# Message layer: destinations, and edge features of five tiles a group, held in PSUM

## The reference, cut to what matters

```
msg  = relu(x[src] + edge_attr)                 # 100000 x 96
aggr = segment_sum(msg, dst, num_segments=3125)
h    = x + aggr
h    = relu(h @ W1 + b1) @ W2 + b2
return x + relu(h)
```

## Time and profile before

| | us |
|---|---|
| median of three runs | 3176.62 |
| profiled execution | 3170.49 |
| its span | 3168.8 |
| first to last indirect gather of the message layer (starts) | 1474.7 to 2173.4 |
| GpSimd busy in those 539 gathers | 535.6 |
| VectorE busy between 1600 and 1700 us | 86.7 |
| TensorE busy in the same 100 us | 93.8 |

### The profile page before, as it was taken

The page is one execution under the profiler, slowest core; times in us unless marked ns, Lnnn a source line. Parts: engine busy times, 40 slices in busy tenths (PEclk is TensorE's granted clock), DMA queues, the critical chain, the costliest instruction groups (busy, mean ns, idle before and its releaser), DMA issues.

```text
span 3168.8 us, 72113 instructions
## 1 busy us (share of the span) xinstructions
PE 2675.9 (84%) x25058; PEld 2208.0 (70%) x25059; DVE 2367.4 (75%) x6307; ACT 640.5 (20%) x1255; POOL 1206.4 (38%) x1205
## 2 busy tenths in 40 slices
PE   4677777889999997996999999997689888888884
PEld 1222222789999997995999999997567677666663
DVE  7888877853332356448888888887799999999986
ACT  0011222510000005011111111111233333333331
POOL 0000000000000000003777777773477777777771
PEclk9999999899999998997999999998799999999996
DMA  1000000000000000003544444441333333333330
GB/s 30 0 0 0 0 0 0 2 1 2 2 1 2 2 2 5 2 1 81 130 120 117 119 116 117 119 115 38 95 103 107 102 107 108 104 104 109 102 98 19
DMA packets 108153, 180.74 MB, mean 57 GB/s; under 512 B 36346, under 2 KB 69900, under 8 KB 107867
## 3 DMA queue, kind: packets, MB, share of 16 engines
q0 software_dynamic: 47824, 89.19, 11.4%
q1 hardware_dynamic: 60043, 87.59, 9.8%
HBM read 171.88 MB, written 4.80 MB: 56 GB/s over the span
## 4 chain that ended last, share of the span: by engine, by line
POOL 34%; issue 11%; DVE 5%; PE 2%; DMA 1%; ACT 0%; DVEq 0%; POOLq 0%; ACTq 0%
POOL gate_rows L1417 20%; POOL msg_rows L1046 14%; DVE pre_space L1120 2%; PE msg_sums L1242 1%; DMA first_rows<-pre_space 0%; DVE msg_rows L1144 0%; DVE pre_space L1540 0%; PE gate_sums L1671 0%; DMA msg_rows<-h_rows,all_src_i 0%; PE msg_sums L1257 0%; ACT msg_src_near L1058 0%; DMA msg_src_row<-src_rows 0%; DVE pre_space L1212 0%; DVE msg_rows L1140 0%; DVE msg_t L1199 0%
## 5 line engine op out<-in xcount | busy, mean ns | idle before, releaser
L1417 POOL DMA_INDIRECT gate_rows<-first_rows,all_src_i x637 | 648.8, 1019 | 198.3 <-issue 193.8
L1046 POOL DMA_INDIRECT msg_rows<-h_rows,all_src_i x539 | 535.6, 994 | 164.1 <-issue 163.8
L1242 PE MATMUL msg_sums<-pre_parts,pre_space 125*128 125x192 f16 x6125 | 531.2, 248 | 37.8 <-DVE pre_space L1120 37.7
L1033 POOL MEMSET pre_middle<- 125x1 f32 x1 | 0.1, 99 | 1465.7 <-POOLq L677 1465.7
L605 PE MATMUL hop_sums<-dense_work,dense_counts 125*128 125x192 f16 (+1 forms) x6250 | 531.7, 247 | 20.5 <-DVE dense_work L569 8.2
L605 PEld LDWEIGHTS hop_sums<-dense_work,dense_counts 125*128 125x128 f16 x6250 | 528.6, 98 | 23.6 <-DVE dense_work L569 10.0
L1242 PEld LDWEIGHTS msg_sums<-pre_parts,pre_space 125*128 125x128 f16 x6125 | 512.3, 99 | 44.8 <-DVE pre_space L1120 39.2
L1646 PE MATMUL gate_sums<-pre_space,pre_parts 125*96 125x384 f16 x2450 | 448.1, 343 | 5.5 <-DVE pre_parts L1514 5.5
L439 PE MATMUL cnt_sums<-cnt_hot,cnt_near 128*128 x1000 | 338.9, 407 | 109.9 <-DVE cnt_hot L371 109.3
L1120 DVE TENSOR_SCALAR pre_space<-msg_src_near,pre_node_no 125x640 f16<-125x640 f16 x1225 | 393.4, 394 | 11.5 <-ACT msg_src_near L1058 11.4
L1646 PEld LDWEIGHTS gate_sums<-pre_space,pre_parts 125*96 125x96 f16 x2450 | 309.2, 129 | 133.0 <-issue 28.8
(11 more groups left out here) (276 smaller groups left out, 3163.5 us busy)
## 6 DMA issues: line engine op xcount, KB each, us to landing
msg_edge<-edges SPq DMA_DIRECT2D x98, 384.0 KB
msg_src_row<-src_rows SPq DMA_DIRECT2D x49, 312.5 KB
gate_edge<-edges SPq DMA_DIRECT2D x98, 128.0 KB
gate_rows<-first_rows,all_src_i POOLq DMA_INDIRECT x637
gate_src_row<-on_src SPq DMA_DIRECT2D x49, 187.5 KB
msg_rows<-h_rows,all_src_i POOLq DMA_INDIRECT x539
gate_inputs<-on_edges SPq DMA_DIRECT2D x49, 48.0 KB, 2.2
first_rows<-pre_space SPq DMA_DIRECT2D x6, 375.0 KB
```

The source lines that it names most:

```text
L1046: nc.gpsimd.indirect_dma_start(out=rows[:, r, k, :], out_offset=None, in_=table, in_offset=bass.IndirectOffsetOnAxis(ap=src_i[:, at:at + 1 ...
L1242: last = nc.tensor.matmul(got[group % 2][:, n, 0:2 * D], pick[:, c % 2, j, i * EP:(i + 1) * EP], parts[:, j, :], start=(j == 0), stop=(j = ...
L1417: nc.gpsimd.indirect_dma_start(out=rows[:, r, k, :], out_offset=None, in_=table, in_offset=bass.IndirectOffsetOnAxis(ap=src_i[:, at:at + 1 ...
```

## The change

Two operands of VectorE's instructions are put into PSUM:

1. The destination numbers of all 784 tiles, as float32, are converted a second time, into banks 6 and 7 (`targets_ps`). The comparison (L1168 before) takes its second input from there; the first, the node numbers, stays in SBUF.
2. Before each group, ScalarE copies the edge features of the first five tiles into bank 5 (`edge_ps`, 480 columns). The addition (L1144 before) takes them from there. In even groups, which have six DMA'd tiles, the sixth keeps its features in SBUF and gets an addition of its own. There is one `edge_ps`, so the copy for the next group waits for this group's addition (`added`), and the addition waits for the copy (`copied`).

```diff
+COPIED = 5
@@ message_layer
+        targets_ps = sums[:, 6:8, :].rearrange("p b w -> p (b w)")[:, 0:ET]
+        edge_ps = sums[:, 5, 0:COPIED * D].rearrange("p (k d) -> p k d", d=D)
@@ scalar
+            def copy_edges(group):
+                act.wait_ge(edge_ready[group % EDGES], 16 * (group // EDGES + 1))
+                nc.scalar.activation(edge_ps, edge[:, group % EDGES, 0:COPIED, :], ACT.Copy).then_inc(copied, 1)
+
+            copy_edges(0)
             widen(1)
             for group in range(NG):
                 r = group % RING
                 act.wait_ge(added, group + 1)
+                if group + 1 < NG:
+                    copy_edges(group + 1)
                 act.wait_ge(placed, group + 1)
                 nc.scalar.activation(rows[:, r, :, :], rows[:, r, :, :], ACT.Relu).then_inc(sent, 1)
@@ vector
             link(nc.vector.tensor_copy(dst_f[:, :], dst_i[:, :]))
+            link(nc.vector.tensor_copy(targets_ps, dst_i[:, :]))
@@ add_edges
-                nc.vector.tensor_tensor(rows[:, r, 0:k, :], rows[:, r, 0:k, :], of_edges[:, 0:k, :],
+                dve.wait_ge(copied, group + 1)
+                if k > COPIED:
+                    nc.vector.tensor_tensor(rows[:, r, COPIED:k, :], rows[:, r, COPIED:k, :], of_edges[:, COPIED:k, :],
+                                            ALU.add)
+                nc.vector.tensor_tensor(rows[:, r, 0:COPIED, :], rows[:, r, 0:COPIED, :], edge_ps,
                                         ALU.add).then_inc(added, 1)
@@ make_onehots
-                    targets = dst_f[:, group * GT:(group + 1) * GT].unsqueeze(2).to_broadcast([EP, GT, SPAN])
+                    targets = targets_ps[:, group * GT:(group + 1) * GT].unsqueeze(2).to_broadcast([EP, GT, SPAN])
```

More of the change, by code:

```diff
@@ L981, in message_layer @@
         edge_ready = [m.sem(f"edge_ready{r}") for r in range(EDGES)]
-        added = m.sem("added"); sent = m.sem("sent"); rows_free = m.sem("rows_free"); all_summed = m.sem("all_summed")
+        copied = m.sem("copied"); added = m.sem("added"); sent = m.sem("sent"); rows_free = m.sem("rows_free"); all_summed = m.sem("all_summed")
         numbered = m.sem("numbered"); row_loaded = [m.sem(f"row_loaded{i}") for i in range(2)]
```

## The result

| us | before | after |
|---|---|---|
| median of 5 runs each, on one chip | 3177.91 | 3161.76 |
| lowest to highest | 3165.95 to 3185.21 | 3152.14 to 3162.33 |
| profiled execution | 3170.49 | 3152.14 |
| its span | 3168.8 | 3150.0 |
| first to last indirect gather of the message layer (starts) | 1474.7 to 2173.4 | 1476.2 to 2152.7 |

The ratio of the runs is 0.9935, with an interval from 0.992 to 0.995: the change saves 0.65% of the time, some 20 us. The two medians by themselves lie 16.2 us apart. Forecast were 3157 for the median and 3151.3 for the profiled execution. The difference is above what can be told from no change, 0.5%, but not by much.

A forecast was written before the change was run, and what follows sets the result against it. GpSimd's unbroken message-layer gathers bound the kernel, VectorE close behind; VectorE's pair of 13.56 - 0.03 + 0.02 + 0.14 + 0.05 = 13.74 us saves 19.2 us: 3151.3 profiled, 3157 median, range 3146 to 3176, chance 0.57.

The forecast's parts named there:

- Stops: Message-layer gathers held by VectorE instructions with two SBUF inputs: 24.5 us at most; GpSimd's stretch shrinks by about 22 us.
- The rival of wide writing: Gathers are stopped by VectorE writing wide float32 results, not by second inputs: no gain, 3177 us; chance 0.11.
- The sum leaves it out: Picks on VectorE might also stop gathers; left out because one gather under them took 0.94 us.
- Reading from PSUM: VectorE's comparison and addition with a PSUM operand: extra cost taken as 0, upper bound twice the length.
- The first rival: VectorE pays for PSUM accesses or the uncovered extra instruction: pair 13.9 to 13.95 us, 3166 us; chance 0.25.
- One more instruction: Extra 96-column addition in 49 even groups, hidden by VectorE's idle on "issue": 0.02 us taken, 0.07 to 0.17 uncovered.
- ScalarE's copy: Copy of 480 columns takes 0.60 us; through Relu and widening it delays VectorE's picks 0.14 us a pair.
- Clock: TensorE's stretches at 1.2 GHz instead of 2.4 show in VectorE's loop: 0.05 us a pair.
- The sum: VectorE's pair of groups 13.74 us against 14.17; over 47 pairs, less 0.95 at the start, 19.2 us saved.
- The lead: GpSimd starts 9 us ahead of VectorE's addition, loses 3 us over 47 pairs, and isn't caught.
- Start: Second conversion of 784 columns on VectorE, between its picks, delays group 0 by 0.95 us (0.55 to 1.2).
- Slower: Rival: new PSUM forms run at half rate, pair 14.72 us, +26 us, 3202 us; decides from 0.5 us a pair; chance 0.07.

The follow-up runs named there:

- changed kernel again: The changed kernel without further edits, run on the same chip as the kernels with only one of its two parts: 3155.36 us, ratio 0.9942 to the kernel before.
- The parts alone: Changed kernel cut to one operand in PSUM: only destination numbers 3159.4 us, ratio 0.9961; only edge features 3163.84 us, ratio 0.997 to the kernel before.
- PSUM dose: Changed kernel plus one unread 512-column comparison in each group, its second input in PSUM: 3156.46 us, one execution.
- SBUF dose: Changed kernel plus one unread 512-column comparison in each group, both inputs in SBUF: 3201.44 us, one execution.
- two copies: Changed kernel with ScalarE's copy of edge features done twice per group, first into unread SBUF: 3181.75 us, ratio 1.0035 to the kernel before.
- the destinations alone: Changed kernel with only the destination numbers in PSUM, edge features left in SBUF, no ScalarE copies: 3159.4 us, ratio 0.9961 to the kernel before.
- the edge features alone: Changed kernel with only five tiles' edge features in PSUM, destinations read from SBUF, no second conversion: 3163.84 us, ratio 0.997 to the kernel before.
- the late copy: Changed kernel with ScalarE's copy placed behind Relu and widening, and ScalarE making the second conversion: 3150.97 us, ratio 0.9935 to the kernel before.
- the gated layer's new one-hots: Changed kernel with late copy and second widening before first copy; gated one-hots as eight 64-column instructions and a small addition: 3320.76 us, ratio 1.0466 to kernel before.

## Why the prediction was right, point by point

*Stops.* Right in cause and size: 22.1 us saved of a forecast "about 22", with 9 gathers of over 1.0 us where there were 84 (22 in the changed kernel again). The parts alone give 11.5 and 11.0; the doses differ by 53.5 us for one operand, 14 of them directly. The rival of wide writing falls by the PSUM dose.

*"The sum leaves it out": picks.* The forecast set aside the half of the Trainium skill's rule ("SBUF — State Buffer", Who interferes with whom) by which an instruction in a two-port mode blocks too, on the ground of one gather of 0.94 us under picks. For the sum of this change that held. As a statement on the chip it was wrong: in the SBUF dose and in the gated layer trains of picks hold a gather for 3.35 and 3.73 us. No row says whether picks run in such a mode; if they do, the rule agrees with these holds. That in the changed kernel's message layer 300 gathers start under picks and none takes over 1.1 us, it doesn't tell, and I had taken that for innocence. A row of the kernel before spoke against it, too. The conversion of the earlier trace rows has one SBUF input, and the gather that starts 0.23 us into it is stopped until 0.83 us after its end. Timeline of GpSimd, 1486 to 1488 us:

```profile
1486.50 1.15 POOL L1046 DMA_INDIRECT msg_rows<-h_rows,all_src_i  x1 [0.30 <-issue]
```

*Reading from PSUM.* Right: 0. The Trainium skill's overheads ("Perfetto Trace Analysis", Optimizing Scalar/DVE Operations), 60 against 125 ns, aren't seen in 688 against 690 and 639 against 640 ns. The first rival (the forecast once calls it the second) falls with it.

*One more instruction.* Right, and by more than I claimed. The idle before L1172 shrank (0.32 against 0.37) and covered it; the PSUM dose shows cover for its 0.67 us.

*ScalarE's copy.* Its length was forecast at 0.60 us and measured at 0.575. In the picks' wait it costs 0.08 us a pair (0.33 against 0.25), not 0.14. The two copies confirm the path: the second puts 0.49 us more into the picks' wait.

*Clock.* The 0.05 us a pair was not there in the first execution. Windows of the changed kernel, in the columns of the earlier trace rows:

```profile
1600.00:1700.00 100.00, 96.98 (x1161) 96.03 (x1159) 90.77 (x269) 23.74 (x35) 75.93 (x80) 1.00 0.48 126
```

TensorE is busy for 96.98 us of 100, against 93.84, and the granted clock is 1.00, against 0.98: from 1520 to 2160 us the stretches at 1.2 GHz are gone, in both executions of the changed kernel. TensorE also waits less for picks (29.8 us in the layer's gathers L1258, against 37.7). A term that I had taken from before over into after was one that went away with the change. What is left of it stands at the start, where the granted clock is 0.91 between 1480 and 1520 us: in the changed kernel again VectorE waits 0.79 us for TensorE in the first pair, 0.02 us a pair.

*The sum.* The pair was forecast at 13.74 and is 13.707, but of other parts. A pair of the kernel before in which nothing held VectorE, timeline 1520 to 1534 us:

```profile
1520.08 0.34 DVE L1140 TENSOR_TENSOR msg_rows<-msg_sums,msg_edge 128x192 f32<-128x192 f32 x1
...
1533.55 0.34 DVE L1140 TENSOR_TENSOR msg_rows<-msg_sums,msg_edge 128x192 f32<-128x192 f32 x1
```

It takes 13.47 us. The forecast's 13.56 was a mean over five pairs, of which three took 13.61 to 13.63, with 16 picks in 5.16 to 5.19 us instead of 5.06: it had held picks in it already, about 0.09 a pair. From 13.47, less 0.02 for an addition that is no longer held (0.76 against 0.74), plus 0.08 for the picks' wait, a free pair of the changed kernel comes to 13.53, as its rows show. On top come 0.23 us in half of the pairs and 0.52 in five, 0.17 on average: some 0.13 of picks held by gathers, and 0.04 of the longer idles of the five. So the forecast had half of this last term, without knowing it, in its base, and terms for copy and clock that were too large by 0.11 together. That the sum agrees to 0.03 is partly luck.

*The lead.* Wrong by its size, and right in what follows by little. The forecast counted from the gather's end on GpSimd and took all 9 us for lead. The waits of the changed kernel again show that 4.9 to 5.3 us of it are the rows' way into SBUF, so some 4 to 5 us could be lost. By the forecast's measure it shrinks from 10.2 to 6.2 us in the first execution, which was enough. In the second it was used up from group 72 on, and VectorE waited 3.5 us. That the mean pair is the same all the same I put down to the two clocks' being level: GpSimd's 11 gathers need 13.76, VectorE's mean pair is 13.71.

*Start.* Forecast 0.95, measured 1.2. The conversion took 1.01 from start to start; the rest is the train of 16 picks behind it, 5.21 us where it was 5.03. The widening, though it stands behind a copy that waits for edge features, was done at 1488.50, before these picks were due; the kernel with the destinations alone, which has no copy, loses the same 1.2. Where the conversion is out of the way, as with the edge features alone and with the late copy, this wait does come through (0.37 and 0.52 us). That it stood ahead of the widening could have been read from the diff.

*Slower.* The rival of half-rate forms has no row for it: none of the new forms in the loop is slower than its neighbour in SBUF. Only the conversion is (0.98 us into PSUM, 0.55 into SBUF), once, and the forecast had counted it so. Its point of decision was sound, though: with 0.60 us more in a pair the two copies land at 1.0035, about where the kernel before is.

## What to carry to other kernels

Where one engine bounds a stage and its instructions' mean lies above their median, line up the long ones with what the other engines do at that moment: moving one operand to another memory can shorten them without touching them. Before removing such a stop, count the second engine's loop to a tenth of a us, since it takes over as the bound, and put what is added where that loop idles anyway. Test such an edit in the stage where it is meant to work: a change of phase can turn gathers that nothing held into stops of 3 us.

## What the runs showed of the hardware that was not expected

- A train of VectorE's picks can hold an indirect gather on GpSimd for the whole train: 3.35 us (ending 0.12 us after the last pick) and 3.73 us (ending 0.8 after), against 0.94. It depends on the phase: with the SBUF dose 254 of the 264 gathers that start under picks take less than 1.1 us, with the gated layer's new one-hots 42 of 122.
- The reverse exists too: nine picks take 3.11 us when they start 0.49 us after a gather's start, and 2.89 when they start 0.78 after. The held pick ends 1.09 us after the gather's start. A GpSimd MEMSET of 2.78 us holds a pick for 2.93.
- The layer's first gather takes 2.67 us in every kernel. It starts under VectorE's 2400-column instruction L1135, whose inputs are both in SBUF. In the changed kernel, timeline 1475 to 1477 us:

```profile
1475.27 2.66 DVE L1135 SCALAR_TENSOR_TENSOR pre_parts<-all_h,pre_parts 125x2400 f16<-125x2400 f32 x1 [3.09 <-ACT pre_parts L1063]
...
1476.23 2.67 POOL L1049 DMA_INDIRECT msg_rows<-h_rows,all_src_i  x1 [0.17 <-issue]
```

It ends at 1478.90, 0.97 us after that instruction's end (1477.93). That is the 0.8 to 1.0 us of the other stops, so I take it for one of them, and not for a cost of being first, as the forecast had it when it took 1.7 us off the stops. No run changes L1135 to show it.
- An instruction of 0.67 us put into each of 98 groups, 66 us of VectorE's work, cost 2.8 us, since VectorE idled on "issue" at that place anyway.
- The same conversion of 784 columns takes 0.55 us into SBUF (L1141) and 0.98 into PSUM (L1142), both in the changed kernel.
